# A recurrence with routed experts on one core: moving the small work behind 24 products in one piece

## The chip, the cores and the metric

The kernel runs on one core of a Trainium2 chip. The metric is the device time of one execution in microseconds. Five engines work side by side, each in the order of its own program, and wait for each other by semaphores: TensorE (PE, with its weight loads as PEld), VectorE (DVE), ScalarE (ACT), GpSimd (POOL) and SyncE (SP), which issues DMAs here.

## The reference

x has 4 sequences of 2048 tokens with 512 features. In short:

```python
xn = layernorm(x)                                # eps 1e-5
h_t = h_{t-1} * A + xn_t                          # along each sequence
s = einsum('sbd,do->bso', h, BC)                  # 512 x 512
chosen = argmax(einsum('bsh,eh->bse', xn, gate_w))  # one of 8 experts
g = silu(xn + expert_w[chosen] @ xn)
out = x + s * g
```

## The kernel before, in words

**First stage.** The 8192 tokens are 32 groups of 256 (two tiles of 128). For each group VectorE takes statistics (`statistics`, `variance`), ScalarE the root (`root`), VectorE the reciprocal with a correction in five small steps (`deviation`, the last of which gives `shift_ready`), and ScalarE normalises in place (`normalise`, one call for each tile, L565). TensorE transposes the group into `ps_xt` (`turn_x`, L976), VectorE scans the four blocks of 128 features along the tokens (`scan`, L724), and each value is split in a high part (ScalarE, `high_part`, L586) and a low part (GpSimd, `low_part`, L424). TensorE multiplies them with BC in 24 products of 128x128 by 512: 16 for the high part (`product_hi`, L1029 and L1030) and 8 for the low one (`product_lo`, L1036). ScalarE copies the two sums out (`take_s`, L600) and SyncE stores them in `token_rows`.

**Routing.** ScalarE copies the transposed group to `xnt` in two halves: `copy_tail` (L572, also before the second half of the scan) and `copy_head` (L576, after its first half). TensorE computes gate scores in parts (`score_parts`, L987), ScalarE copies them (`copy_parts`, L581), TensorE turns them (`scores`, L995). VectorE's `route(c)` finds the expert of each token; step by step between its own operations it holds the five steps of `deviation` of the group two further and the two steps of `place(c - 1)` (L757, L762), which give the slots of the group before (`slot_ready`). TensorE counts the ranks (`ranks`, L1004 to L1011). GpSimd scatters token numbers to those slots by two indirect DMAs (`scatter_ids`, L442).

**Weights.** Beside this, one block of the experts' weights in each group is loaded (SyncE, `load_w`, after the turning two blocks before), the identity is added on its diagonal (GpSimd, `add_identity`, L410, `w_ready`), VectorE turns it (`turn_w`, L808, `wt_done`), and it is split (`block_high` L590, `block_low` L814).

**Second stage.** The tokens are gathered by expert in 71 tiles, multiplied with the weights, gated and scattered. The change doesn't touch it.

**The order in a group** is written out by hand for each engine. In the group c of the first stage, with offsets saying for which group a step is:
- VectorE: scan c+1, low block c-1, statistics and variance c+3, turn_w c, route c+1 (with deviation c+3 and place c).
- ScalarE: high block c-1, tail and head copy c+1, sums c-1 out, high part c+1, normalise c+2 first tile, score parts c+1, normalise c+2 second tile, root c+3.
- TensorE: turn x c+1, 16 high products c, score parts c+1, 8 low products c, scores c+1, ranks c.
- GpSimd: count c, low part c+1, ids c+1, scatter c, add_identity c+1.
- SyncE: load of x c+4, store of x c+3, load of weights c+2, store of sums c.

`turn_w(c)` waits for `w_ready` of c + 1, which GpSimd gives behind the scatter of c-1; the scatter waits for `slot_ready`:

```python
pool.wait_ge(slot_ready, 4 * it + c + 1)      # scatter_ids, L440
...
dve.wait_ge(w_ready, c + 1)                   # turn_w, L806
```

The last three groups (TAIL = 29 and behind) have an order of their own.

Of the kernel before, what the change touches and what calls it, by code (L numbers as in the profile page):

```python
# [35 lines left out]
def bass_recurrent_routed(nc, x_in, a_in, bc_in, gate_in, expert_in, out):  # L36
# [5 lines left out]
    TPG = 2  # L42
# [21 lines left out]
    TAIL = GROUPS - 3  # L64
# [17 lines left out]
    with ExitStack() as ctx:  # L82
        def sb(name, shape, dt):
            return ctx.enter_context(nc.sbuf_tensor(name, shape, dt))
# [93 lines left out]
        first = sb("first", [P, TPG], F32)  # L178
# [372 lines left out]
        def _(act):  # L551
            def root(it, c):

                act.wait_ge(var_ready, 4 * it + c + 1)
                wait(act, shift_ready, 4 * it + c)
                nc.scalar.activation(std2[:, :], mv[:, c % 4, :, 1], ACT.Sqrt, bias=eps_col[:, 0:1],
                                     scale=4.0).then_inc(std_ready, 1)

            def normalise(it, c, t):

                if t == 0:
                    wait(act, x_stored[c % XR], 16 * (rounds(4, it, c, XR) - (1 if c % XR < XR - 1 else 0) + 1))
                    act.wait_ge(shift_ready, 4 * it + c + 1)
                xt = x_sb[:, c % XR, t]
                nc.scalar.activation(xt, xt, ACT.Identity, bias=shift[:, c % 2, t:t + 1],  # L565
                                     scale=mv[:, c % 4, t, 1:2]).then_inc(xn_ready, 1)
# [11 lines left out]
            def copy_parts(it, c):  # L578
                act.wait_ge(part_done, 4 * it + c + 1)
                wait(act, score_done, 4 * it + c)  # L580
                nc.scalar.copy(score_sb[:, :], part_ps).then_inc(part_copied, 1)  # L581

            def high_part(it, c):
                act.wait_ge(scan_done, CH * (4 * it + c + 1))
                wait(act, s_done, TPG * (4 * it + c - 1))
                nc.scalar.copy(hs_hi[c % 2], hs[:, c % 2]).then_inc(hi_done, 1)  # L586
# [40 lines left out]
            def group(it, c, start=False):  # L627
                if not start:
                    block_high(0, c - 1)
                copy_tail(it, c + 1)  # L630
                copy_head(it, c + 1)
                if not start:
                    take_s(it, c - 1)
                if start:
                    copy_parts(0, 1)
                high_part(it, c + 1)
                normalise(it, c + 2, 0)
                if not start:
                    copy_parts(it, c + 1)
                normalise(it, c + 2, 1)  # L640
                root(it, c + 3)

            for c in range(TAIL):
# [47 lines left out]
        def _(dve):  # L691
# [19 lines left out]
            def scan(it, c, between=False):  # L711
                n = U * it + c
                v = c % 2
                dve.wait_ge(xt_done, n + 1)
                wait(dve, lo_done, n - 1)
                wait(dve, scan_done, CH * n)
                for k in range(CH):
                    if k == CH // 2:
                        if between:
                            place(it, c - 1, 0)  # L720
                            place(it, c - 1, 1)
                        dve.wait_ge(xnt_tail, n + 1)
                    start = 0.0 if c % GPB == 0 else hs[:, 1 - v, k, GT - 1:GT]
                    nc.vector.tensor_tensor_scan(hs[:, v, k, :], a_col[:, k:k + 1].to_broadcast([P, GT]),  # L724
                                                 xt_ps[:, k, :], start, ALU.mult, ALU.add).then_inc(scan_done, 1)
# [38 lines left out]
            def route(it, c, ahead, behind=True):  # L764


                n = U * it + c
                v = c % 2
                if ahead:
                    deviation(it, c + 2, 0)  # L770
                dve.wait_ge(score_done, n + 1)
                if behind:
                    place(it, c - 1, 0)
                points = bank_score if n < 3 or n > TAIL else score
                order = bank_score if n > TAIL else ranked
                nc.vector.tensor_reduce(points[:, :, :], score_ps.rearrange("p t k e -> p t e k"), AX.X,
                                        ALU.add).then_inc(gate_step, 1)
                if behind:
                    place(it, c - 1, 1)
                dve.wait_ge(gate_step, 5 * n + 1)  # L780
                nc.vector.tensor_reduce(top[:, :], points[:, :, :], AX.X, ALU.max).then_inc(gate_step, 1)
                if ahead:
                    deviation(it, c + 2, 1)
                dve.wait_ge(gate_step, 5 * n + 2)
                for t in range(TPG):
                    last = nc.vector.scalar_tensor_tensor(order[:, t], points[:, t], top[:, t:t + 1],
                                                          prio[:, t], ALU.is_equal, ALU.mult)
                last.then_inc(gate_step, 1)
                if ahead:
                    deviation(it, c + 2, 2)  # L790
                dve.wait_ge(gate_step, 5 * n + 3)
                nc.vector.tensor_reduce(first[:, :], order[:, :, :], AX.X, ALU.max).then_inc(gate_step, 1)
                if ahead:
                    deviation(it, c + 2, 3)
                dve.wait_ge(gate_step, 5 * n + 4)
                wait(dve, rank_done, n - 1)
                wait(dve, seen_ready, n - 1)
                for t in range(TPG):
                    last = nc.vector.tensor_scalar(onehot[:, v, t], order[:, t], first[:, t:t + 1], None,
                                                   ALU.is_equal)  # L800
                last.then_inc(onehot_ready, 1)
                if ahead:
                    deviation(it, c + 2, 4)

            def turn_w(c):
                dve.wait_ge(w_ready, c + 1)  # L806
                wait(dve, w_lo_done, c)
                nc.vector.transpose(w_blocks, w_stage[:, c % WR].rearrange("p (i k r) -> p i k r", i=CH, r=Q)  # L808
                                    ).then_inc(wt_done, 1)

            def block_low(it, c):
                n = U * it + c
                dve.wait_ge(w_hi_done, n + 1)
                nc.vector.tensor_tensor(block_of(w_lo, U // CH * it, c), w_turned, block_of(w_hi, U // CH * it, c),  # L814
                                        ALU.subtract).then_inc(w_lo_done, 1)
# [23 lines left out]

            def group(it, c, start=False):  # L840
                scan(it, c + 1)
                if not start:
                    block_low(0, c - 1)
                if start:
                    for step in range(5):
                        deviation(0, 2, step)
                statistics(it, c + 3)
                dve.wait_ge(stats_done, U * it + c + 4)
                wait(dve, mv_taken, U * it + c)
                wait(dve, id_ready, U * it + c)  # L850
                dve.sem_inc(mv_free, 1)
                variance(it, c + 3)
                turn_w(c)
                route(it, c + 1, True)

            for c in range(TAIL):
                group(0, c, start=(c == 0))
            dve.wait_ge(table_empty, 16)
            scan(0, TAIL + 1, between=True)
            block_low(0, TAIL - 1)  # L860
            turn_w(TAIL)
# [105 lines left out]
        def _(pe):  # L967
# [86 lines left out]
            score_parts(0, 0)  # L1054
            scores(0, 0)

            def group(it, c, first=False):
                if first:
                    product_hi(it, c, 0, first=(c == 0))
                    turn_x(it, c + 1)  # L1060
                    product_hi(it, c, 1)
                    product_lo(it, c, 0)
                    score_parts(it, c + 1)
                else:
                    turn_x(it, c + 1)
                    product_hi(it, c, 0)
                    product_hi(it, c, 1)
                    score_parts(it, c + 1)
                    product_lo(it, c, 0)
                product_lo(it, c, 1)  # L1070
                scores(it, c + 1)
                ranks(it, c)

            for c in range(4):
                group(0, c, first=(c < 2))
            with pe.Fori(1, GROUPS // 4 - 1) as it:
                for c in range(4):
                    group(it, c)
            group(0, TAIL - 1)
            a, b, c = TAIL, TAIL + 1, TAIL + 2  # L1080
            turn_x(0, b)
            product_hi(0, a, 0)
# [100 lines left out]
```

## Time and profile before

| | us |
|---|---|
| three runs | 510.81, 511.56, 511.59 |
| median | 511.56 |
| profiled execution | 511.46 |
| its span | 509.7 |
| TensorE busy in it | 490.1 (96%) |
| VectorE busy | 409.7 (80%) |
| GpSimd busy | 323.2 (63%) |
| ScalarE busy | 260.1 (51%) |

All times below are microseconds from the start of the span. A timeline row has the start, the duration, the engine, the line, the operation with what it writes and reads, and a count; a bracket at its end gives the idle time of the engine just before it and what ended it ("issue" where the profile shows nothing that was waited for). Operations of one engine overlap a little, so the distance of two starts is often shorter than a duration. The groups of the first stage follow each other with almost the same times from about 50 to 235; one of them is shown for each engine.

### The profile page before, as it was taken

Reading aid. Unit: us, or ns where it says so; the run is one execution under the profiler, and the core shown is the slowest. Engines: PE = TensorE matmul, PEld = TensorE weight load, DVE = VectorE, ACT = ScalarE, POOL = GpSimd, SP = SyncE. Lnnn points to the kernel's source line nnn. Section 1 sums busy time; section 2 is a strip of 40 time slices with the busy share of each in tenths; the row PEclk is TensorE's granted clock in tenths of the full one; section 3 lists DMA queues with packets and bytes.
Section 4 is the critical chain, followed back from the end, with each engine's and each line's share of the span. In section 5 each row is a group of like instructions: output and inputs, shape, how many; then the busy total and the mean of one; then the engine's idle time right before and its main releaser. Section 6 shows DMA issues by size and latency. Waiting matters only on the chain. (4 is left out here: it accounts for less than half of the span.)

```text
span 509.7 us, 10779 instructions
## 1 busy us (share of the span) xinstructions
PE 490.1 (96%) x2722; PEld 383.3 (75%) x2723; DVE 409.7 (80%) x1077; ACT 260.1 (51%) x500; POOL 323.2 (63%) x390
## 2 busy tenths in 40 slices
PE   7989999999999999999988999999999999999993
PEld 6667777777777777777766888888888888887782
DVE  5989999999899899999854887777777777767672
ACT  4676876776776776786532333333333333332330
POOL 2567667667667766777544667676666666666652
PEclk9999999999999999999999999999999999999998
DMA  7979678778778878776346677777777776767620
GB/s 235 351 254 278 216 259 265 223 252 257 233 245 254 246 235 250 245 240 207 109 136 250 218 246 225 228 238 260 237 229 229 227 238 216 234 186 232 212 84 9
DMA packets 65523, 114.53 MB, mean 225 GB/s; under 512 B 9914, under 2 KB 27962, under 8 KB 65488
## 3 DMA queue, kind: packets, MB, share of 16 engines
q1 hardware_dynamic: 47328, 62.46, 39.2%
q0 software_dynamic: 18160, 51.72, 31.9%
q14 instruction: 26, 0.21, 0.1%
q8 instruction: 9, 0.15, 0.1%
HBM read 66.21 MB, written 55.08 MB: 238 GB/s over the span
## 5 line engine op out<-in xcount | busy, mean ns | idle before, releaser
L1134 PE MATMUL ps_s<-w_hi,split 128*128 x284 | 118.4, 417 | 0.7 <-DVE split L929 0.4
L679 ACT ACTIVATE ps_s<-ps_s 128x512 f32<-128x512 f32 x71 | 41.3, 582 | 149.2 <-PE ps_s L1136 149.2
L526 POOL DMA_INDIRECT out_dram<-work x71 | 73.8, 1039 | 65.7 <-DVE work L942 54.1
L1135 PE MATMUL ps_s<-w_lo,split 128*128 x284 | 112.3, 396 | 0.0
L1136 PE MATMUL ps_s<-w_hi,split 128*128 x284 | 112.3, 395 | 0.0
L1029 PE MATMUL ps_s<-bc_hi,split 128*128 128x512 f32 x256 | 104.4, 408 | 0.7 <-ACT split L586 0.6
L424 POOL TENSOR_TENSOR split<-work,split 128x1024 fp32r<-128x1024 f32 x30 | 72.7, 2423 | 45.6 <-ACT split L586 45.6
L1030 PE MATMUL ps_s<-bc_lo,split 128*128 128x512 f32 x256 | 101.3, 396 | 0.0
L508 POOL DMA_INDIRECT work<-token_rows,work x70 | 74.9, 1070 | 28.4 <-issue 27.4
L442 POOL DMA_INDIRECT slot_table<-token_id,slot_id x64 | 63.5, 992 | 28.6 <-issue 24.5
L724 DVE TENSOR_TENSOR_SCAN work<-a_col,work,ps_xt 128x256 f32<-128x256 f32 x112 | 74.4, 722 | 0.0
L922 DVE TENSOR_SCALAR work<-work 128x512 f32<-128x512 f32 x70 | 38.7, 553 | 37.7 <-DMA work<-token_rows,work 36.8
L1036 PE MATMUL ps_s<-bc_hi,split 128*128 128x512 f32 x256 | 68.5, 408 | 0.0
L929 DVE TENSOR_TENSOR split<-ps_xt,split 128x512 fp32r<-128x512 f32 x71 | 48.9, 688 | 19.9 <-ACT split L674 19.6
L1136 PEld LDWEIGHTS ps_s<-w_hi,split 128*128 128x128 f32 x284 | 53.4, 188 | 12.6
L1134 PEld LDWEIGHTS ps_s<-w_hi,split 128*128 128x128 f32 x284 | 53.7, 189 | 12.0 <-issue 2.4
L1036 PEld LDWEIGHTS ps_s<-bc_hi,split 128*128 128x128 f32 x256 | 45.6, 188 | 21.1 <-issue 11.9
L1135 PEld LDWEIGHTS ps_s<-w_lo,split 128*128 128x128 f32 x284 | 53.6, 189 | 9.7
L1029 PEld LDWEIGHTS ps_s<-bc_hi,split 128*128 128x128 f32 x256 | 48.2, 188 | 11.8 <-issue 0.9
L1030 PEld LDWEIGHTS ps_s<-bc_lo,split 128*128 128x128 f32 x256 | 48.3, 189 | 9.9
L565 ACT ACTIVATE work<-work,shift,mv 128x512 f32<-128x512 f32 x64 | 52.9, 833 | 2.2 <-DMA token_rows<-work 1.2
L942 DVE TENSOR_TENSOR work<-work 128x512 f32<-128x512 f32 x71 | 49.2, 693 | 2.4
(125 smaller groups left out, 730.9 us busy)
## 6 DMA issues: line engine op xcount, KB each, us to landing
token_rows<-work SPq DMA_DIRECT2D x31, 528.0 KB, 3.2
work<-in_L_attn_inputs_dram SPq DMA_DIRECT2D x31, 512.0 KB, 4.8
token_rows<-work SPq DMA_DIRECT2D x29, 512.0 KB, 5.5
work<-in_L_ffn_expert_w_dram SPq DMA_DIRECT2D x128, 64.0 KB, 4.0
slot_table<-w_lo SPq DMA_DIRECT2D x1, 2080.0 KB, 13.5
token_rows<-in_L_attn_inputs_dram SPq DMA_DIRECT2D x3, 512.0 KB, 10.9
out_dram<-work POOLq DMA_INDIRECT x71, 3.3
work<-token_rows,work POOLq DMA_INDIRECT x70, 4.5
```

The lines of the kernel that those rows point to most:

```text
L424: nc.gpsimd.tensor_tensor(hs_lo[c % 2], hs[:, c % 2], hs_hi[c % 2], ALU.subtract).then_inc(lo_done, 1)
L442: nc.gpsimd.indirect_dma_start(out=table_flat, out_offset=bass.IndirectOffsetOnAxis(ap=slot_id[:, u, t:t + 1], axis=0), in_=token_id[:, c ...
L508: nc.gpsimd.indirect_dma_start(out=row_sb[:, u], out_offset=None, in_=rows, in_offset=bass.IndirectOffsetOnAxis(ap=tok, axis=0), bounds_ch ...
L526: nc.gpsimd.indirect_dma_start(out=out_flat, out_offset=bass.IndirectOffsetOnAxis(ap=slot_tok[:, n:n + 1], axis=0), in_=o_sb[:, u], in_off ...
L565: nc.scalar.activation(xt, xt, ACT.Identity, bias=shift[:, c % 2, t:t + 1], scale=mv[:, c % 4, t, 1:2]).then_inc(xn_ready, 1)
L724: nc.vector.tensor_tensor_scan(hs[:, v, k, :], a_col[:, k:k + 1].to_broadcast([P, GT]), xt_ps[:, k, :], start, ALU.mult, ALU.add).then_inc ...
L1029: nc.tensor.matmul(ps_s[:, 2 * v + t], left, bc_hi[:, k], start=(k == 0), stop=False)
L1030: nc.tensor.matmul(ps_s[:, 2 * v + t], left, bc_lo[:, k], start=False, stop=False)
L1036: last = nc.tensor.matmul(ps_s[:, 2 * v + t], hs_lo[v][:, k, t * P:(t + 1) * P], bc_hi[:, k], start=False, stop=(k == CH - 1))
L1134: nc.tensor.matmul(z_ps[v], hi, wh, start=(k == 0), stop=False)
L1135: nc.tensor.matmul(z_ps[v], hi, wl, start=False, stop=False)
L1136: last = nc.tensor.matmul(z_ps[v], lo, wh, start=False, stop=(k == CH - 1))
```

## The change

- TensorE, groups 4 to 27 (`group_together`): 16 high and 8 low products of the group without anything between them, then the score parts of c+1, then the turning of x of c+2 (before: of c+1, ahead of the products), then scores c+1 and ranks c. One `turn_x(0, 5)` is put ahead of the loop; group 28 has its old order without the turning, which is done already.
- ScalarE, groups 4 to 27: the copy of the score parts goes behind the second tile's normalisation.
- VectorE, from group 4 on: the route is that of c, not c+1, and stands directly behind the scan of c+1 (group 4 has none); `turn_w(c)` stands behind the low block, ahead of statistics. The route of 29 is put behind the last group, ahead of the scan of 30.
- GpSimd and SyncE are as before.

```diff
@@ ACT group @@
+                together = 4 <= c < TAIL - 1
                 high_part(it, c + 1)
                 normalise(it, c + 2, 0)
-                if not start:
+                if not start and not together:
                     copy_parts(it, c + 1)
                 normalise(it, c + 2, 1)
+                if together:
+                    copy_parts(it, c + 1)
                 root(it, c + 3)
@@ DVE group @@
                 scan(it, c + 1)
+                if c > 4:
+                    route(it, c, True)
                 if not start:
                     block_low(0, c - 1)
+                if c >= 4:
+                    turn_w(c)
...
                 variance(it, c + 3)
-                turn_w(c)
-                route(it, c + 1, True)
+                if c < 4:
+                    turn_w(c)
+                    route(it, c + 1, True)
 
             for c in range(TAIL):
                 group(0, c, start=(c == 0))
             dve.wait_ge(table_empty, 16)
+            route(0, TAIL, True)
             scan(0, TAIL + 1, between=True)
@@ PE @@
+            def group_together(it, c):
+                for t in range(TPG):
+                    product_hi(it, c, t)
+                for t in range(TPG):
+                    product_lo(it, c, t)
+                score_parts(it, c + 1)
+                turn_x(it, c + 2)
+                scores(it, c + 1)
+                ranks(it, c)
+
             for c in range(4):
                 group(0, c, first=(c < 2))
+            turn_x(0, 5)
             with pe.Fori(1, GROUPS // 4 - 1) as it:
                 for c in range(4):
-                    group(it, c)
-            group(0, TAIL - 1)
+                    group_together(it, c)
+            group(0, TAIL - 1, turned=True)
```

## Rows read from the trace of the kernel before

**Rows 1.** The page: its span, and TensorE's granted clock in 40 slices.
```profile
span 509.7 us, 10779 instructions
...
PEclk9999999999999999999999999999999999999998
```
**Rows 2.** Timeline of TensorE, one period: start, duration, engine, line, operation, count.
```profile
123.62 0.48 PE L1029 MATMUL ps_s<-bc_hi,split 128*128 128x512 f32 x1
123.93 0.40 PE L1030 MATMUL ps_s<-bc_lo,split 128*128 128x512 f32 x1
...
127.20 0.40 PE L1030 MATMUL ps_s<-bc_lo,split 128*128 128x512 f32 x1
127.53 0.64 PE L987 MATMUL ps_gate<-xnt,gate_col 128*32 128x256 f32 x8
...
130.38 1.07 PE L976 MATMUL ps_xt<-ident,work 128*128 128x128 f32 x8
131.21 0.48 PE L1029 MATMUL ps_s<-bc_hi,split 128*128 128x512 f32 x1
```
**Rows 3.** Timeline of VectorE, the same period.
```profile
122.94 0.17 DVE L734 RECIPROCAL half<-std 128x2 f32<-128x2 f32 x1 [0.45 <-ACT std L556]
...
123.26 0.16 DVE L762 TENSOR_REDUCE slot_id<-placed 128x2 int32<-128x16 f32 x1
...
124.60 2.65 DVE L724 TENSOR_TENSOR_SCAN work<-a_col,work,ps_xt 128x256 f32<-128x256 f32 x4
127.17 0.67 DVE L814 TENSOR_TENSOR w_lo<-ps_w,w_hi 128x512 fp32r<-128x512 f32 x1
127.75 1.28 DVE L702 BATCH_NORM_STATS2 stats<-work 128x6 f32<-128x512 f32 x2
129.20 0.25 DVE L708 BATCH_NORM_AGGREGATE mv<-stats 128x2 f32<-128x6 f32 x2 [0.17 <-DVE stats L702]
129.37 0.69 DVE L808 STREAM_TRANSPOSE ps_w<-work 128x512 f32<-128x512 f32 x1
130.51 0.17 DVE L734 RECIPROCAL half<-std 128x2 f32<-128x2 f32 x1 [0.45 <-ACT std L556]
```
**Rows 4.** Timeline of GpSimd, the same period.
```profile
124.28 1.01 POOL L442 DMA_INDIRECT slot_table<-token_id,slot_id  x1 [0.50 <-issue]
...
126.59 0.47 POOL L410 TENSOR_TENSOR work<-work,ident 128x128 f32<-128x128 f32 x1
...
128.69 2.40 POOL L424 TENSOR_TENSOR split<-work,split 128x1024 fp32r<-128x1024 f32 x1 [1.46 <-ACT split L586]
```
**Rows 5.** Timeline of all engines, a scatter that GpSimd waited for.
```profile
32.41 0.16 DVE L762 TENSOR_REDUCE slot_id<-placed 128x2 int32<-128x16 f32 x1
...
33.43 1.01 POOL L442 DMA_INDIRECT slot_table<-token_id,slot_id  x1 [1.17 <-DVE slot_id L762]
```
**Rows 6.** Timeline of ScalarE, the period of rows 2.
```profile
126.01 0.59 ACT L576 COPY xnt<-ps_xt 128x512 f32<-128x512 f32 x1 [1.53 <-DVE work L724]
126.49 0.20 ACT L595 COPY work<-mv 128x4 f32<-128x4 f32 x1
...
130.18 0.30 ACT L556 ACTIVATE std<-mv,eps_col 128x2 f32<-128x2 f32 x1
130.37 0.59 ACT L590 CAST w_hi<-ps_w 128x512 fp32r<-128x512 f32 x1
```
**Rows 7.** Timeline of all engines: first product of group 4, scan of group 30.
```profile
47.70 0.48 PE L1029 MATMUL ps_s<-bc_hi,split 128*128 128x512 f32 x1
...
238.44 1.37 DVE L724 TENSOR_TENSOR_SCAN work<-a_col,work,ps_xt 128x256 f32<-128x256 f32 x2
```
**Rows 8.** The page's costliest groups: count, busy time, mean ns of one.
```profile
L565 ACT ACTIVATE work<-work,shift,mv 128x512 f32<-128x512 f32 x64 | 52.9, 833 | 2.2 <-DMA token_rows<-work 1.2
```
**Rows 9.** Timeline of all engines, a low part beside VectorE's subtraction at the start.
```profile
13.84 1.22 DVE L833 TENSOR_TENSOR bc_lo<-work,bc_hi 128x1024 fp32r<-128x1024 f32 x1
14.02 3.28 POOL L424 TENSOR_TENSOR split<-work,split 128x1024 fp32r<-128x1024 f32 x1 [2.15 <-ACT split L586]
```

More of the change, by code:

```diff
@@ L1055, in _, with group @@
             scores(0, 0)
-            def group(it, c, first=False):
+            def group(it, c, first=False, turned=False):
                 if first:
@@ L1064, in group @@
                 else:
-                    turn_x(it, c + 1)
+                    if not turned:
+                        turn_x(it, c + 1)
                     product_hi(it, c, 0)
```

## The prediction, made before the changed kernel ran

> **What bounds the kernel now.** I read the page first (span, slices, clock), then the timeline of each engine over one steady period, then the waits. The page gives a span of 509.7 us and TensorE's clock at the full level in all but the last slice [rows 1], so nothing here turns on the clock. The profiled execution took 511.46 us, 1.76 around the span, and lies 0.10 under the median of 511.56; the sum is made against 511.46.
>
> TensorE's timeline shows one group of 256 tokens in 131.21 - 123.62 = 7.59 us, without a wait between its instructions [rows 2]. VectorE's period is the same (130.51 - 122.94 = 7.57), but 0.45 of it is a wait for ScalarE's root, so its own work is 7.0 to 7.1: from the start of the scan 2.57 to the next operation, then 0.58 for the low block, 1.45 statistics, 0.17 variance, about 0.61 turning of weights (0.69 less the overlap of 0.08 that the low block has with its successor: 0.67 long, the next starts 0.58 behind), and 1.66 route (122.94 to 124.60); the sum is 7.04 [rows 3]. So TensorE sets the pace, and VectorE has 0.5 to spare. GpSimd never keeps anybody waiting in these groups. That last point is where the change bites: the reader should look at when GpSimd's two scatters start.
>
> **GpSimd's chain, as it is now.** The scatter of a group's slots waits for `slot_ready`, which the second step of `place` (L762) gives. L762 ends at 123.26 + 0.16 = 123.42, the first scatter starts at 124.28: 0.86 later [rows 3, 4]. Is that the wait or GpSimd's own work? At 33.43 the row names VectorE's slot_id as the releaser; GpSimd had been idle for 1.17 and L762 ended at 32.41 + 0.16, again 0.86 before [rows 5]. So 0.86 is release to start. From the first scatter's start to `add_identity` (L410) is 126.59 - 124.28 = 2.31, and L410 takes 0.47 [rows 4]. From the end of L762 to weights with their diagonal is 0.86 + 2.31 + 0.47 = 3.64 us, in GpSimd's program order. Now VectorE turns these weights only at 129.37 [rows 3], 2.3 us after L410's end, so the chain is free.
>
> **The change, part by part.**
>
> TensorE: the 24 products run in one piece. Product to product is (127.20 - 123.93)/14 = 0.234; from the last product to the score parts 0.33, so leaving the products costs 0.10 [rows 2]. One such exit of two goes: 7.49 a group, a gain of 0.10, 2.4 us over 24 groups, if TensorE stays the bound. The turning of x is moved by most of a group; it issues the same eight passes.
>
> ScalarE: the copy of the score parts goes behind the second normalisation. The same operations; it costs nothing while ScalarE ends its group before the variance, which the loop below leaves room for (score parts are wanted by TensorE only behind the turning of x).
>
> VectorE, turning weights ahead of statistics: same durations, but see below. The route of group c+1 becomes the route of group c, behind the scan of c+1. It holds `place(c-1)` and the deviation of c+2. The route also takes its waits: scores and ranks come from TensorE's previous group, root from ScalarE's previous group, all ready by the scan's end.
>
> The new wait is at `turn_w(c)`. It needs `add_identity(c)`, which GpSimd's program has behind `scatter_ids(c-1)`, which needs `place(c-1)`. Before, `place(c-1)` was in VectorE's previous group; now it is in the same group, just ahead of `turn_w(c)`. So VectorE waits for a chain that it released itself a moment ago, in every group from 5 to 28. Queued behind that wait on VectorE are statistics, variance and the next scan; for the scan wait the head copy, high part, products and the next route.
>
> Period of this loop, from one scan's start S to the next:
> - scan to first step of the route 2.57; to L762 0.32; L762 0.16: S + 3.05 [rows 3]
> - release to first scatter 0.86; to L410 2.31; L410 0.47: S + 6.69 [rows 4, 5]
> - GpSimd's semaphore to VectorE: no row shows VectorE waiting for GpSimd. The nearest is ScalarE's root to VectorE, 130.48 to 130.51, 0.03 [rows 3, 6]; bounds 0 and 0.1, I take 0.05
> - turning 0.61, statistics 1.45, variance 0.17 [rows 3]: next scan at S + 8.97.
>
> VectorE's own work beside the 3.64 chain is the rest of the route (124.60 - 123.42 = 1.18) and the low block 0.58, so it idles for 3.64 + 0.05 - 1.76 = 1.93: 7.04 + 1.93 gives the same 8.97.
>
> A second, small wait comes with it. The variance now comes directly before the next scan, and ScalarE's root, which waits for it, has the block copy and the tail copy of the next group queued behind it. Variance ends 0.25 - 0.17 = 0.08 behind the scan's start; 0.05 to the root; 0.19 root to block copy; 0.48 for one copy to the next; 0.59 for the tail copy; 0.05 back: S + 1.44 [rows 6]. The scan's second half wants it at half of 2.65, S + 1.33. That is 0.11 more: **9.08 us a period**. Bounds of this term: 0, if ScalarE runs ahead, and 0.3.
>
> Is any other loop longer? Deviation done at S + 2.57 + 1.66 + 0.08 = 4.3, two normalisations of 0.83 to 6.0 [rows 8], the second half of the transposes (half of 1.07 [rows 2]) and a release to 6.6: below 8.97. TensorE needs 7.49. GpSimd's other work fits today into 7.59 - 3.64 = 3.95, so it is done by S + 10.6, and its next slots come at S + 12.1: room. SyncE's four weight loads wait for the turning but have a whole group before L410 needs them. So TensorE idles about 1.6 a group, in front of the turning of x or of the score parts.
>
> **The sum.** Group 4 has no route on VectorE, so the scan of 6 waits for TensorE alone: products from 47.70 [rows 7], 3.91 + 8 x 0.234 = 5.78, parts 0.64, transposes 1.07 [rows 2]: it starts at 55.2. Then 24 periods (groups 5 to 28) of 9.08 = 217.9, then the route of 29 that is now ahead of the scan of 30, 1.66: the scan of 30 starts at 274.8. Before it started at 238.44 [rows 7]. Shift 36.3. Behind that scan both kernels have the same order, and its head copy, score parts and plan hang on it, so I carry the shift to the end unchanged (bounds -1.5, if TensorE's work piled up at the end is less, and +1). 511.46 + 36.3 = **547.8 us**.
>
> **Rivals.**
> - *The intended gain.* If the chain through GpSimd did not stand between place and turning (if it took under 1.76 us from L762's end, the point from which it decides, instead of 3.64), TensorE would set 7.49 a group: 511.46 - 2.4 = 509.1, with up to 1 more at the start. For it: VectorE's 7.04 and the 6.6 loop lie below. Against: the program order of GpSimd, and the 0.86 in both cases shown. 5%.
> - *A chain partly hidden.* If the 0.86 were mostly preparation that GpSimd does while it waits longer, and L410 started sooner, the period would be about 8.3: 55.2 + 24 x 8.3 + 1.66 = 256.1, a shift of 17.6, 529 us. Against it: at 33.43 GpSimd had idled for 1.17 and still took 0.86 [rows 5]. 6%.
> - *GpSimd is slowed by what it now runs beside.* Scatters and L410 move from beside the scan to beside the route and the low block. The low part that took 3.28 ran beside a subtraction of two SBUF tensors on VectorE (1.22) [rows 9]; one in the steady stretch takes 2.40 [rows 4]. At the difference of 0.88 more a group the period is 9.96: 55.2 + 239.0 + 1.66 = 295.9, shift 57.5, 569 us. Of VectorE's work in the scatters' stretch only a few steps of some 0.15 read two SBUF tensors; at 0.15 a group it adds 3.6 (551.4), which the range holds. 6% for more than the range.
>   The Trainium skill, GPSIMD Engine Reference, section Key points, says that GpSimd shares its SBUF interfaces with VectorE, and that VectorE instructions with two SBUF inputs or in a 2-port mode contend for them. By that rule, which the row of 3.28 agrees with, this rival's price is the small one (551.4), and without it the forecast stays as it is.
> - *The change does not do what it says:* products stay in one piece, but TensorE waits elsewhere in each group. That is part of the forecast, no case of its own.
>
> **How the numbers follow.** Forecast mechanism (GpSimd's chain in VectorE's loop, period 8.8 to 9.25): 81%. Intended gain 5%; a gain at the start of the groups and a small wait that cancel 2%; partly hidden 6%; longer 6%. Period 8.8 with the tail's -0.5 gives 540.6, period 9.25 with +1 gives 552.9; I take 541 to 553, which leaves out about 2 in 10. A measurement of this kernel can tell 0.2% from no change, some 1 us. Faster 0.05, same 0.02, slower 0.93.
>
> **What would show it.** In the changed kernel's waits: VectorE's turning of weights waiting for GpSimd's `add_identity` 24 times, about 1.9 each, some 45 us; VectorE's scans 9.08 apart; the first scatter still 0.86 behind `place`; TensorE with idle time of 1.5 a group; the tail copy just late for the scan's second half. Wrong: scans 7.5 apart, or the weights turned without a wait, or the wait there but of another length (then the 0.86 or the 2.31 changed).

## The result, and the profile after

| | us |
|---|---|
| kernel before, median of 5 | 511.30 (510.81 to 511.59) |
| changed kernel, median of 5 | 546.85 (546.71 to 547.68) |
| ratio, 95% interval | 1.0704 (1.0689 to 1.0720) |
| profiled execution, its span | 546.71, 545.0 |

The kernel became 7.0% slower, 35.5 us. 547.8 was forecast, with a range of 541 to 553. Some executions of any of these kernels fall into a slower state: the medians of the experiments below hold every execution, the ratios leave those out.

The page of the changed kernel, its head and the groups in which the time went: line, engine, operation, count, then busy time and mean ns, then the idle time of the engine just before it and what ended most of that.

```profile
span 545.0 us, 10785 instructions
...
PE 502.3 (92%) x2722; PEld 388.1 (71%) x2723; DVE 411.5 (76%) x1077; ACT 262.1 (48%) x500; POOL 322.1 (59%) x390
...
PEclk9999999999999999999799999999999999999997
...
L442 POOL DMA_INDIRECT slot_table<-token_id,slot_id x64 | 63.5, 992 | 71.7 <-DVE slot_id L765 58.4
...
L811 DVE STREAM_TRANSPOSE ps_w<-work 128x512 f32<-128x512 f32 x32 | 23.1, 723 | 43.8 <-POOL work L410 43.4
```

VectorE's busy time is that of before within 2 us (411.5 against 409.7), GpSimd's within 1.1 (322.1 against 323.2). TensorE has the same 2722 instructions; its idle time rose by 23.1 and its busy time by 12.2 (502.3 against 490.1). Passes overlap less where TensorE stops between them (a product has 0.40 in its row and its successor starts 0.23 behind it), which may be why; it was not taken apart. What is new is a row that the kernel before did not have: VectorE's turning of weights (now L811) has idle time of 43.8 us before it, 43.4 of it for GpSimd's identity (L410), and of the 71.7 before GpSimd's scatter (L442) 58.4 is for VectorE's slots (now L765). Two engines that wait for each other in turn are the mark of a loop.

VectorE's timeline over one period of the changed kernel answers [rows 3]:

```profile
145.44 2.67 DVE L727 TENSOR_TENSOR_SCAN work<-a_col,ps_xt 128x256 f32<-128x256 f32 x4
148.03 0.14 DVE L737 RECIPROCAL half<-std 128x2 f32<-128x2 f32 x1
...
148.29 0.16 DVE L765 TENSOR_REDUCE slot_id<-placed 128x2 int32<-128x16 f32 x1
...
149.63 0.68 DVE L817 TENSOR_TENSOR w_lo<-ps_w,w_hi 128x512 fp32r<-128x512 f32 x1
152.12 0.73 DVE L811 STREAM_TRANSPOSE ps_w<-work 128x512 f32<-128x512 f32 x1 [1.81 <-POOL work L410]
152.75 1.24 DVE L705 BATCH_NORM_STATS2 stats<-work 128x6 f32<-128x512 f32 x2
154.17 0.25 DVE L711 BATCH_NORM_AGGREGATE mv<-stats 128x2 f32<-128x6 f32 x2 [0.17 <-DVE stats L705]
154.34 2.79 DVE L727 TENSOR_TENSOR_SCAN work<-a_col,work,ps_xt 128x256 f32<-128x256 f32 x4
```

and GpSimd's answers [rows 4]:

```profile
149.31 1.01 POOL L442 DMA_INDIRECT slot_table<-token_id,slot_id  x1 [2.45 <-DVE slot_id L765]
150.63 0.97 POOL L442 DMA_INDIRECT slot_table<-token_id,slot_id  x1 [0.31 <-issue]
151.61 0.47 POOL L410 TENSOR_TENSOR work<-work,ident 128x128 f32<-128x128 f32 x1
```

Read the two together: L765 ends at 148.45; 0.86 later the first scatter starts; 2.30 later L410; it ends at 152.08; VectorE turns at 152.12, 0.04 behind. Then 2.22 to the next scan. The scan of 154.34 is followed by the next at 163.34, 9.00 later. In before the same engines had the same durations, but VectorE asked for the weights 2.3 us after they were ready.

### The profile page after: what moved, and what is told of

Its sections match the earlier page's. It is cut to its first block and busy times, and to the rows that moved or that the text cites. A ratio compares the mean times of both kernels' runs of the same rounds, so it can differ in the third digit from the quotient of the medians.

```text
span 545.0 us, 10785 instructions
## 1 busy us (share of the span) xinstructions
PE 502.3 (92%) x2722; PEld 388.1 (71%) x2723; DVE 411.5 (76%) x1077; ACT 262.1 (48%) x500; POOL 322.1 (59%) x390
## 5 line engine op out<-in xcount | busy, mean ns | idle before, releaser
L442 POOL DMA_INDIRECT slot_table<-token_id,slot_id x64 | 63.5, 992 | 71.7 <-DVE slot_id L765 58.4
L727 DVE TENSOR_TENSOR_SCAN work<-a_col,work,ps_xt 128x256 f32<-128x256 f32 x112 | 76.7, 731 | 1.1 <-PE ps_xt L985 0.6
L1045 PEld LDWEIGHTS ps_s<-bc_hi,split 128*128 128x128 f32 x256 | 48.5, 192 | 14.0 <-issue 2.5
L1038 PEld LDWEIGHTS ps_s<-bc_hi,split 128*128 128x128 f32 x256 | 48.0, 188 | 12.1 <-issue 0.9
L811 DVE STREAM_TRANSPOSE ps_w<-work 128x512 f32<-128x512 f32 x32 | 23.1, 723 | 43.8 <-POOL work L410 43.4
L565 ACT ACTIVATE work<-work,shift,mv 128x512 f32<-128x512 f32 x64 | 49.2, 810 | 12.0 <-DVE shift L752 12.0
```

Source lines behind the costliest of these rows:

```text
L442: nc.gpsimd.indirect_dma_start(out=table_flat, out_offset=bass.IndirectOffsetOnAxis(ap=slot_id[:, u, t:t + 1], axis=0), in_=token_id[:, c ...
L1038: nc.tensor.matmul(ps_s[:, 2 * v + t], left, bc_hi[:, k], start=(k == 0), stop=False)
L1045: last = nc.tensor.matmul(ps_s[:, 2 * v + t], hs_lo[v][:, k, t * P:(t + 1) * P], bc_hi[:, k], start=False, stop=(k == CH - 1))
```

## The experiments

The experiments set two theories against each other: the forecast's (place, two scatters, identity and turning form a chain that VectorE waits for), and a rival, that the order of the route or of TensorE's work costs the time whatever GpSimd does. Each ratio is to the kernel before on the same chip; where one is turned into microseconds it is times 511.3. The period is the distance of the starts of two scans of VectorE.

**Identity ahead of the scatter.** One exchange cuts the chain:

```diff
                 next_ids(it, c + 1)
-                scatter_ids(it, c)
                 add_identity(it, c + 1)
+                scatter_ids(it, c)
```

> The changed kernel with one exchange in GpSimd's group: the identity of block c+1 is added ahead of the scatter of c. Nothing else differs. Theory (the turning of weights waits for place, two scatters and the identity, in that order): the chain is cut, VectorE's turning no longer waits, TensorE sets the pace with 7.49 us a group instead of 9.0, and the time falls by 24 x 1.51 = 36.2 to about 510.6 us, a little below the kernel before. Rival (the route behind the scan makes TensorE wait for onehot and for the normalised x, whatever GpSimd does): scans stay 9.0 apart and the time stays at 546 to 547.

Measured: median 513.48, ratio 1.0017 (0.9985 to 1.0050), against 1.0704 with the order of the change. Of the loss of 35 us 0.9 is left (by the interval, between -0.8 and 2.6), and all that was changed is the order of the same work on GpSimd. VectorE's waits in this run between 60 and 235:

```profile
DVE work L727 <- PE ps_xt L985: 5.2, 15, 0.7
...
DVE ps_w L811 <- POOL work L410: 0.2, 1, 0.2
```

The columns are the total, how often, and the longest. The wait for L410, 41.6 us in 23 times between 60 and 265 of the changed kernel, is left once, with 0.2; VectorE now waits for TensorE. So the rival falls. But the period is 7.58, not the 7.49 that was expected, and the time 512.2 by the ratio, not 510.6; the section on the reasons comes back to that.

**Identity between the two scatters.** The chain is one scatter shorter.

```diff
                 for t in range(TPG):
+                    if between and t == 1:
+                        add_identity(it, c + 1)
                     nc.gpsimd.indirect_dma_start(
```

> The changed kernel with the identity added between the two scatters of a group. Theory: the chain is shorter by one scatter, from start to start 1.31 us, so the period is 9.0 - 1.31 = 7.69 and the time 546.9 - 24 x 1.31 = 515.4. A rival in which GpSimd's chain isn't what sets the period expects 546 to 547, or, if any shortening were enough for another bound at 8 us or above, more than 523.

Measured: median 517.94, ratio 1.0090 (1.0053 to 1.0128), which is 515.9 against 515.4 expected; the period is 7.75 against 7.69 expected. VectorE still waits, 0.55 a group, and that is the rest of the chain:

```profile
142.16 0.16 DVE L766 TENSOR_REDUCE slot_id<-placed 128x2 int32<-128x16 f32 x1
144.72 0.73 DVE L812 STREAM_TRANSPOSE ps_w<-work 128x512 f32<-128x512 f32 x1 [0.55 <-POOL work L410]
```

**One GpSimd operation more in the chain.**

```diff
                 scatter_ids(it, c)
+                nc.gpsimd.tensor_tensor(spare[:, c % 4], ident[:, :], ident[:, :], ALU.add)
                 add_identity(it, c + 1)
```

> The changed kernel with one more GpSimd addition of 128x128 (result unused) between the second scatter and the identity of each group. Like the identity it takes 0.47 and the next operation starts 0.41 behind it. Theory (everything from place to the turning of weights is on the path): 28 groups have it, 24 of them in the loop, so 24 x 0.41 = 9.9 more than 546.9: 556.8. Rival (GpSimd has slack somewhere, the loop is closed by another wait): less than 3 more.

Measured: 556.27, ratio 1.0867 (1.0827 to 1.0908). That is 0.0163 x 511.3 = 8.3 more than the changed kernel. The added operation moves L410 by 0.36, not 0.41:

```profile
145.34 0.42 POOL L462 TENSOR_TENSOR spare<-ident 128x128 f32<-128x128 f32 x1
145.70 0.47 POOL L411 TENSOR_TENSOR work<-work,ident 128x128 f32<-128x128 f32 x1
```

and 24 x 0.36 = 8.6. The period went from 9.01 to 9.36. (29 groups have the operation, not 28; that does not touch the sum.)

**The same operation outside the chain**, behind the scatters with the identity ahead of them:

```diff
                 add_identity(it, c + 1)
                 scatter_ids(it, c)
+                nc.gpsimd.tensor_tensor(spare[:, c % 4], ident[:, :], ident[:, :], ALU.add)
```

> The changed kernel with the identity ahead of the scatters and the same unused addition of 0.47 in each of GpSimd's groups, now behind the scatters. Theory (GpSimd's work counts only where it stands between place and the turning of weights): nothing on top of the 513.5 of the identity ahead alone, within 1.5. Rival (GpSimd as a whole is the bound): 24 x 0.4 = 9.6 more, 523.

Measured: 514.25, ratio 1.0068 (1.0043 to 1.0092). The period stays 7.58 and the profiled execution took 512.82, against 513.12 without the operation. The ratio is 0.5% above that of the identity ahead alone, 2.6 us, and the two intervals just overlap; whether a part of that is real stays open. It is a little over a quarter of the 9.6 that the rival wants.

**The turning of weights at its old place**, the rest as changed:

```diff
-                if c >= 4:
-                    turn_w(c)
...
                 variance(it, c + 3)
+                turn_w(c)
                 if c < 4:
-                    turn_w(c)
                     route(it, c + 1, True)
```

> The changed kernel with the turning of weights back behind the variance; route, TensorE and ScalarE as changed. Theory: behind place VectorE then has the rest of the route, low block, statistics and variance, 1.18 + 0.58 + 1.45 + 0.17 = 3.38 us, before it asks for the weights, against GpSimd's 3.64 + 0.05: it waits 0.3, its period is 7.04 + 0.3 = 7.35, below TensorE's 7.49, and the time is about 510.6. Rival (the place of the route alone costs the time): 547.

Measured: 513.16, ratio 1.0023 (0.9986 to 1.0061). The period is 7.59. So the early route and the new TensorE order cost nothing that can be told if the turning comes late enough. The 3.38 of VectorE's own work all but covers the 3.64: between 60 and 235 the wait for L410 is left 11 times, with 3.4 in all.

**Only the turning moved**, on the kernel before:

```diff
                     block_low(0, c - 1)
+                if c >= 4:
+                    turn_w(c)
...
                 variance(it, c + 3)
-                turn_w(c)
+                if c < 4:
+                    turn_w(c)
                 route(it, c + 1, True)
```

> The kernel before with only the turning of weights moved ahead of statistics from group 4 on; the route stays at the end of VectorE's group. Theory: place of the group before is then a whole scan ahead of the turning, GpSimd's chain ends 3.64 us behind it, at about 2.5 after the scan's start, and the turning comes at 3.15: no wait, 511.3 within 1. Rival (turning ahead of statistics costs by itself, by delaying statistics, variance and root): root 0.6 later and so up to 24 x 0.6 = 14 us more, 525.

Measured: 512.76, ratio 1.0010 (0.9969 to 1.0052); scans mostly 7.65 apart, against 7.57 to 7.60 in before. Neither half of VectorE's change costs anything that can be told in its right company. Together they put `place` and the turning one behind the other in a group, with 1.76 us between them.

**Only the route moved**, on the kernel before (with the early turning left out too):

```diff
                 scan(it, c + 1)
+                if c > 4:
+                    route(it, c, True)
...
                 turn_w(c)
-                route(it, c + 1, True)
+                if c < 4:
+                    route(it, c + 1, True)
```

> The kernel before with only VectorE's route put as in the change (route of c behind the scan of c+1), turning of weights, TensorE and ScalarE as before. Theory: GpSimd's chain is nearly hidden (3.7 against 3.4), but the score parts of c+1, which TensorE has in the middle of its products, wait for onehot of c, 4.6 us behind the group's first product, and 3.68 of TensorE's work follows: a period of 8.2, 24 x 0.64 = 15 more than before, 527. A rival in which the early route costs nothing without the changed turning expects 511 to 513.

Measured: 528.67, ratio 1.0350 (1.0308 to 1.0391), period 8.29. TensorE's row names the wait:

```profile
150.45 0.64 PE L991 MATMUL ps_gate<-xnt,gate_col 128*32 128x256 f32 x8 [0.63 <-DVE onehot L799]
151.02 2.12 PE L1040 MATMUL ps_s<-bc_hi,split 128*128 128x512 f32 x8
```

The score parts stand in front of the 8 low products, which wait behind them. So the early route wants the new TensorE order.

**Only TensorE and ScalarE as changed**, VectorE as before:

```diff
-                if c > 4:
-                    route(it, c, True)
...
-                if c >= 4:
-                    turn_w(c)
...
-                if c < 4:
-                    turn_w(c)
-                    route(it, c + 1, True)
+                turn_w(c)
+                route(it, c + 1, True)
```

> The changed TensorE and ScalarE order alone, VectorE's program as before. Theory: scores of c+1 now come at the end of TensorE's group, VectorE's route of c+1 waits for them and stands ahead of the next scan: root, normalisation and the turning of x end about 6.0 behind the scan's start, scores at 6.4, route 1.6, so 8.1 a period: 24 x 0.52 = 12.5 more than before, 524. Rival (one piece of products is worth 0.1 a group by itself): 509.

Measured: 522.38, ratio 1.0222 (1.0183 to 1.0260), period 8.09. VectorE's waits in it, between 60 and 235, are for the root and for ranks, both in front of the route that stands ahead of the next scan:

```profile
DVE half L737 <- ACT std L556: 10.3, 22, 0.6
DVE placed L760 <- PE ps_gate L1014: 10.0, 22, 0.5
```

So the new TensorE order wants the early route. Either alone loses; both with the chain cut come out even.

**Ranks ahead of scores**, with the identity ahead of the scatter:

```diff
                 turn_x(it, c + 2)
-                scores(it, c + 1)
+                pe.wait_ge(part_copied, 4 * it + c + 2)
                 ranks(it, c)
+                scores(it, c + 1)
```

> The changed kernel with the identity ahead of the scatter, and on TensorE ranks of c ahead of scores of c+1. Behind the turning of x the scores started 0.93 after its first pass, where the products of the kernel before started after 0.83. If the 0.10 is what entering the scores costs behind any TensorE work of full width, it goes when the small rank products stand between, and the period falls from 7.58 to 7.48: 24 x 0.10 = 2.4 less than with the identity ahead alone, about 0.5% . If it belongs to the scores wherever they stand: no change.

Measured: 512.95, ratio 1.0019 (0.9996 to 1.0043), period 7.55. It gained 0.03 a group, not 0.10: a miss. What follows the turning of x still starts 0.93 behind its first pass, ranks as well as scores.

**Group 28 in the new order too**, on top of that (ScalarE's copy of the score parts goes behind the second normalisation there as well; TensorE's edit is shown):

```diff
-            group(0, TAIL - 1, turned=True)
+            group_together(0, TAIL - 1)
             a, b, c = TAIL, TAIL + 1, TAIL + 2
-            turn_x(0, b)
```

> Identity ahead of the scatter, ranks ahead of scores, and group 28 in the new order too on TensorE and ScalarE (before: its score parts stand between the products and wait 0.4 for onehot). The steady groups then take 7.55, but with the identity ahead alone the scan of 30 still started 2.15 later than in the kernel before, since the route of 29 stands ahead of it. Expected: 0.4 to 0.8 less than with ranks ahead alone, 512.3, no better than the kernel before by more than can be told. If all of the loss at the end were TensorE's wait in group 28, 511.

Measured: 513.61, ratio 1.0036 (1.0013 to 1.0059). No gain: the scan of 30 follows that of 29 by 10.16, where it was 9.63 with ranks ahead alone. The loss at the end isn't TensorE's wait in group 28. None of the versions is faster than the kernel before.

## Why the prediction was right, step by step

**The chain through GpSimd: right, and shown.** Its 3.64 from slots to weights measured 0.86 + 2.30 + 0.47 = 3.63. The release from GpSimd to VectorE, taken as 0.05 without a row, is 0.04. In the period shown, whose scan starts a sequence, the loop adds up to 2.59 + 0.26 + 0.16 + 3.63 + 0.04 + 2.22 = 8.90, the measured distance of its scans (145.44 to 154.34). Forecast was 8.97 before the term of the tail copy; without the lateness that the next paragraph finds, a period with an ordinary scan has 2.57 + 0.26 + 0.16 + 3.63 + 0.04 + 2.22 = 8.88. The difference is the route up to L765, 0.26 instead of 0.32.

VectorE's wait was forecast as 1.93 and is 1.81. The chain isn't shorter for it: the forecast took the low block with its distance to the next operation, 0.58, but in front of a wait it counts with all of its 0.68. From the end of L765 to the turning 1.18 + 0.68 + 1.81 = 3.67 go by, which is the chain's 3.63 + 0.04.

**The tail copy late for the scan: right.** The changed kernel's four scans take 2.79 where those of before take 2.65 [rows 3], and ScalarE's root waits for the variance with the copies behind it:

```profile
154.46 0.30 ACT L556 ACTIVATE std<-mv,eps_col 128x2 f32<-128x2 f32 x1 [2.88 <-DVE mv L711]
154.66 0.57 ACT L590 CAST w_hi<-ps_w 128x512 fp32r<-128x512 f32 x1
155.12 0.59 ACT L572 COPY xnt<-ps_xt 128x512 f32<-128x512 f32 x1
```

The tail copy ends at 155.71, 1.37 behind the scan's start, and the scan's third operation starts at 155.74, 1.40 behind it where that was 1.30 in before (124.60 to 125.90). From the scan's start to the route it is 2.70 (154.34 to 157.04), against 2.57: 0.13, forecast 0.11. The period is 9.01, forecast 9.08. The scan that starts a sequence needs no start value and is shorter by itself (2.41 in before against 2.65); the period that begins with it is 8.90.

**The start: 55.60, forecast 55.2.** The forecast counted from a product at 47.70 in before; in the changed kernel's profile that product starts at 48.13, 0.43 later, and the scan of 4, ahead of any change, is 0.55 later already (41.81 against 41.26). The way from that product to the scan took 7.47, forecast 7.49.

**The end: one wait left out.** The scan of 29 starts at 262.39 and that of 30 at 273.79, 11.40 later, where the forecast had 9.08 + 1.66 = 10.74. The route of 29, moved ahead of the scan of 30, waits for a root whose variance directly precedes it; the forecast had costed that route without its wait:

```profile
271.24 0.25 DVE L711 BATCH_NORM_AGGREGATE mv<-stats 128x2 f32<-128x6 f32 x2 [0.17 <-DVE stats L705]
271.92 0.17 DVE L737 RECIPROCAL half<-std 128x2 f32<-128x2 f32 x1 [0.43 <-ACT std L556]
```

The next scan would have followed at 271.41; the reciprocal comes at 271.92, 0.51 later. Another 0.20 is lost to TensorE's clock. The forecast left it out, since before has it at the full level to the last slice, but in this profile the granted clock is 1.00 from 265 to 266, 0.59 from 266 to 267, 0.50 from 272 to 273 and 0.99 from 273 to 274: it was at 1.2 instead of 2.4 GHz for about 7 us, and it fell while TensorE waited 2.61 for the onehot of 28 (264.25 to 266.86). The 8 low products took 3.58 there (267.87 to 271.45) where they take 1.96, the ranks of 28 were ready at 272.11, and the step of `place` that needs them came 0.30 behind the reciprocal instead of 0.10.

**The sum.** 55.60 + 23 x 8.99 + 11.40 = 273.8, against 238.44 in before [rows 7]: 35.4, forecast 36.3. The first filler product behind the first stage (TensorE's products whose result nobody uses) starts at 294.74, against 259.16 in before: 35.6, so the shift is carried to the end as forecast. The three misses, +0.4 at the start, -2.1 in 23 periods and +0.7 at the end, partly cancel; none is large beside the 35.

**What was wrong: the price of the intended gain.** The forecast read that leaving the products costs 0.10 and took the period without the chain as 7.49, the time as 509.1. With the chain cut it is 7.58. TensorE's timeline there, one period:

```profile
147.09 0.48 PE L1038 MATMUL ps_s<-bc_hi,split 128*128 128x512 f32 x1
...
152.86 0.64 PE L996 MATMUL ps_gate<-xnt,gate_col 128*32 128x256 f32 x8
153.43 1.09 PE L985 MATMUL ps_xt<-ident,work 128*128 128x128 f32 x8
154.36 0.34 PE L1004 MATMUL ps_gate<-ident,score_sb 104*128 104x104 f32 x2
...
154.67 0.48 PE L1038 MATMUL ps_s<-bc_hi,split 128*128 128x512 f32 x1
```

The 24 products in one piece take 5.77, 0.11 less than 3.91 + 1.97 in the two pieces of before. The size of that term was right, its place was not. The products are left once in either kernel for the score parts, 0.33 behind the last of them; the last low product of before has the scores 0.23 behind it, like any product, so there was no second exit to save. What goes is a slow start: the first low product behind the score parts has the second 0.34 behind it (128.10 to 128.44), with the products in one piece 0.23 (150.90 to 151.14).

And the turning of x, which now stands between score parts and scores, takes 0.93 to the next operation (153.43 to 154.36), where it took 0.83 between ranks and products [rows 2]. The gain is given back in the same group. The step that failed here is "it issues the same eight passes": the passes are the same, their price depends on their neighbours. The trace shows where most of the 0.10 is, at the last pass. From the sixth pass to what follows the turning it is 0.25 when that is a product (before) and 0.33 when it is the scores (chain cut):

```profile
130.96 0.49 PE L976 MATMUL ps_xt<-ident,work 128*128 128x128 f32 x3
131.21 0.48 PE L1029 MATMUL ps_s<-bc_hi,split 128*128 128x512 f32 x1
...
154.03 0.49 PE L985 MATMUL ps_xt<-ident,work 128*128 128x128 f32 x3
154.36 0.26 PE L1004 MATMUL ps_gate<-ident,score_sb 104*128 104x104 f32 x1
```

It is 0.33 as well when the ranks follow (153.02 to 153.35 with ranks ahead of scores), which is why that experiment left the 0.93; it put one small operation in place of another, not a product. The other 0.02 is at the first pass, which has the second 0.14 behind it when ranks stand ahead and 0.16 when the score parts do. The kernel before had the same order once, near its end: score parts, turning, scores, and 0.93 (241.62 to 242.55). That price could have been read before the change ran. Why a product can follow sooner, no run shows.

With the chain cut the scan of 30 starts 2.15 later than in before (240.59 against 238.44). The scan of 6 is 1.12 earlier (55.25 against 56.37), the 23 periods behind it lose 0.85, and the last step takes 10.01 instead of 7.59, because the route of 29 stands in it behind its variance. That the last step's loss belongs to this route is shown by the runs: it is 10.01 and 10.03 with the route of 29 ahead of the scan of 30 (identity first, turning late), and 7.65 and 7.56 where the route of 29 is at its old place (only the turning moved, only TensorE and ScalarE as changed).

**GpSimd beside other work: the small price, or none.** The scatters take 1.01 and 0.97, as in before [rows 4], L410 0.47. The Trainium skill, GPSIMD Engine Reference, section Key points, names VectorE instructions with two SBUF inputs as contending with GpSimd. In the scatters' new stretch VectorE's longest operation of a route takes 0.43, and its low block reads one of its two inputs from PSUM; no row there shows a cost.

## What to carry to other kernels

Before moving a step on one engine, list what it releases and what it asks for, and follow each through the other engine's program order: here a release and a request that had been a group apart met in one group, with 1.8 us of own work to cover a chain of 3.6. Two reorders that are each free can close a loop together, and the cheapest cure was here on the third engine, which nobody had touched (the identity did not need the scatter; it only stood behind it). The page shows such a loop as two rows of idle time that name each other's engine while busy times stay the same.

## What the runs showed of the hardware that was not expected

- The same eight transposes on TensorE take 0.83 to the next operation between the small rank products and a product of 128x512, and 0.93 between the score parts and the scores. 0.08 of the difference is at the last pass: the product starts 0.03 behind it, scores or ranks 0.11. Between two products of 128x512, at the start of the kernel before, the eight take 0.79 (24.15 to 24.94).
- The first 128x512 product behind the score parts has its successor 0.34 behind it, one that stands behind a product 0.23.
- TensorE's granted clock fell to 1.2 GHz in the middle of the changed kernel, from 266 to 273, in a wait of 2.61; the kernel before, and the one with the identity first, whose wait at this place is 0.39, had no such fall. What sets it off was not tried.
- With the slots given later in GpSimd's group, the next ids wait for the landing of the scatter before: 22.8 us in 22 times between 60 and 265. From issue to landing a scatter took 4.7 in the median, 3.5 in before. It cost nothing here, because GpSimd still waited 2.4 for the next slots behind it.
